# Attention in six groups instead of five, a fourth slot for the sine angles, and new engine orders

## What is computed

```python
y = einsum('bnh,boh->bno', x, weight[subject]) + bias[subject]        # per batch its own weights
q, k, v = heads of y @ Wq.T + bq, y @ Wk.T + bk, y @ Wv.T + bv         # 16 heads of 16
sim = q k^T / sqrt(16) / (|temperature| + 0.1)
scores = sum over 5 frequencies f of alpha[h,f] * sin(2 pi sim / f + phi[h,f])
w = sigmoid(scores); w = w / (sum(w) + 1e-10)
x1 = x + layernorm((w v) @ Wo.T + bo) * gamma + beta
x2 = x1 + relu(x1 @ W1[lang] + b1[lang]) @ W2[lang] + b2[lang]          # adapter per batch
z  = layernorm(x2) * gamma[lang] + beta[lang]
for t in 32 batches:                                                   # recurrence over the batches
    f, i, g = sigmoid(z_t @ wf.T + c @ uf.T + bf), sigmoid(... wi, ui), tanh(... wc, uc)
    c = f * c + i * g
out = x1 + tanh(z @ wo.T + c_final @ uo.T + bo)
```

## Time and profile before

| | |
|---|---|
| Median of 3 runs | 363.52 us (363.08 to 364.91) |
| The profiled execution | 362.38 us, span 360.5 us |
| DVE busy | 302.3 us (84%) |
| PE busy | 296.2 us (82%) |
| ACT busy | 281.9 us (78%) |
| POOL busy | 39.9 us (11%) |
| DMA | 27.55 MB |

### The profile page before, as it was taken

How to read it: one execution, slowest core, us unless ns; L and a number is a source line. 1 busy time by engine, 2 the same in 40 slices (tenths; PEclk the granted TensorE clock), 3 DMA queues, 4 the chain that set the end, 5 groups by cost and what they waited for, 6 DMA issues and landing times.

```text
span 360.5 us, 7287 instructions
## 1 busy us (share of the span) xinstructions
PE 296.2 (82%) x2572; PEld 169.9 (47%) x2572; DVE 302.3 (84%) x661; ACT 281.9 (78%) x407; POOL 39.9 (11%) x49
## 2 busy tenths in 40 slices
PE   5855869577778788798898988998897999998895
PEld 5643348444434455443464545454553434543253
DVE  2379998789988999999799999999999989565344
ACT  1399889599998999999699998999996965322223
POOL 5000930010200001400200011110001301101000
PEclk9999888689989999999899998999999989999999
DMA  6597234553103540034024100220310021000006
GB/s 188 170 276 272 70 91 112 134 154 88 32 18 94 135 141 0 2 96 104 7 73 120 46 4 0 68 64 22 80 38 2 1 86 35 2 0 2 0 12 220
DMA packets 30439, 27.55 MB, mean 76 GB/s; under 512 B 10947, under 2 KB 24387, under 8 KB 30404
## 3 DMA queue, kind: packets, MB, share of 16 engines
q1 hardware_dynamic: 30116, 26.58, 25.4%
q10 hardware_dynamic: 288, 0.53, 0.4%
HBM read 23.16 MB, written 2.10 MB: 70 GB/s over the span
## 4 chain that ended last, share of the span: by engine, by line
DVE 40%; PE 21%; ACT 19%; issue 8%; SPq 7%; POOL 2%; DMA 2%; DVEq 0%; ACTq 0%
DVE sc L1496 12%; ACT ang L1017 6%; DVE ang L1481 5%; PE pg L591 5%; ACT ang L1008 4%; DVE ang L1472 3%; PE pg L584 3%; SPq L295 3%; PE pf L449 2%; PE pr L545 2%; DVE sc L1494 2%; PE pf L507 2%; POOL rs L373 2%; DVE fc L1616 1%; DVE cst L1621 1%
## 5 line engine op out<-in xcount | busy, mean ns | idle before, releaser
L1496 DVE SCALAR_TENSOR_TENSOR sc<-ang,small,sc 128x512 f32<-128x512 f32 (+1 forms) x160 | 98.6, 643 | 1.3
L1017 ACT ACTIVATE ang<-ang,qs 128x2560 f32<-128x2560 int32 x32 | 76.9, 2425 | 1.1 <-DVE ang L1481 0.9
L1008 ACT ACTIVATE ang<-sc,phase 128x512 int32<-128x512 f32 (+1 forms) x126 | 72.5, 641 | 0.0
L584 PE MATMUL pg<-gate_w,zT 128*64 128x384 f32 x256 | 52.5, 519 | 0.9 <-DVE zT L1611 0.9
L591 PE MATMUL pg<-gate_u,cT 128*64 128x384 f32 x256 | 49.6, 510 | 1.8 <-DVE cT L1626 1.8
L1481 DVE TENSOR_SCALAR ang<-ang 128x2560 int32<-128x2560 int32 x32 | 47.7, 1498 | 0.3 <-ACT ang L1008 0.2
L1051 ACT ACTIVATE gat<-pg 128x384 f32<-128x384 f32 x32 | 15.5, 485 | 31.2 <-PE pg L591 31.1
L507 PE MATMUL pf<-qm,kT 64*64 64x128 f32 x512 | 19.9, 298 | 14.0 <-issue 4.5
L1472 DVE TENSOR_SCALAR ang<-sc,phase 128x256 int32<-128x256 f32 (+1 forms) x74 | 28.1, 421 | 1.2 <-ACT sc L999 1.2
L591 PEld LDWEIGHTS pg<-gate_u,cT 128*64 128x64 f32 x256 | 17.5, 142 | 24.3 <-issue 18.4
L584 PEld LDWEIGHTS pg<-gate_w,zT 128*64 128x64 f32 x256 | 16.0, 141 | 20.9 <-issue 17.1
(11 more groups left out here) (125 smaller groups left out, 485.2 us busy)
## 6 DMA issues: line engine op xcount, KB each, us to landing
wc<-in_cond SPq DMA_DIRECT2D x30, 257.0 KB, 3.2
wa<-in_down SPq DMA_DIRECT2D x32, 66.0 KB, 1.9
w<-in_up SPq DMA_DIRECT2D x32, 64.2 KB, 2.2
xt<-in_xt SPq DMA_DIRECT2D x8, 256.0 KB, 3.4
b<-in_up_b SPq DMA_DIRECT2D x32, 64.0 KB, 2.1
out_t<-go SPq DMA_DIRECT2D x8, 256.0 KB, 2.2
xg<-in_x SPq DMA_DIRECT2D x3, 512.0 KB, 4.9
qm<-qT SPq DMA_DIRECT2D x48, 32.0 KB, 2.0
```

Of the source, the lines that this page charges most:

```text
L584: pe.matmul(pg[n % 2][u * L:(u + 1) * L, 0:GCOLS], zT[:, q % 2, kc, t * L:(t + 1) * L], gate_w[:, kc, u, :], start=False, stop=(kc == KC - ...
L1008: op = act.activation(ang[:, n % SLOTS, f, r], unit(n)[:, r], ACT.Identity, scale=TURN / FREQS[f], bias=phase[:, p * NF + f:p * NF + f + 1])
L1017: act.activation(a.bitcast(F32), a, ACT.Sin, scale=2 * PI_LOW / TURN, bias=qs[:, 3:4]).then_inc(sine_ready, 1)
L1496: op = dve.scalar_tensor_tensor(out=unit(n)[:, r], in0=sine, scalar=amp, in1=unit(n)[:, r], op0=ALU.mult, op1=ALU.add)
```

## The change

The third group of 8 batches (20 to 27 of the 32) becomes two groups of 4. SLOTS goes from 3 to 4. ON_ACT falls from 4 to 3 for units 21, 23, 25 and 27. To make room in memory, `rows` loses its fourth plane, `go` keeps only six of eight results and the last two live in `b2` (`kept`). All five lists of calls are new. Of ScalarE's sines and weights, 19 carry True instead of 26.

```diff
-SIZES = (4, 8, 8, 8, 4)
+SIZES = (4, 8, 8, 4, 4, 4)
...
-SLOTS = 3
+SLOTS = 4
...
-ON_ACT = [2, 2, 3, 3, 3, 4, 3, 4, 3, 4, 3, 4, 3, 4, 3, 4, 3, 4, 3, 4, 3, 4, 3, 4, 3, 4, 3, 4, 3, 3, 3, 2]
+ON_ACT = [2, 2, 3, 3, 3, 4, 3, 4, 3, 4, 3, 4, 3, 4, 3, 4, 3, 4, 3, 4, 3, 3, 3, 3, 3, 3, 3, 3, 3, 3, 3, 2]
 ACT_BEFORE = [sum(ON_ACT[:n]) for n in range(B + 1)]
+SPREAD_AT = (0, (GB - SIZES[0]) // PB * PB)
...
-        rows = sb("rows", [P, 4, D])
+        rows = sb("rows", [P, 3, D])
...
-        go = sb("go", [P, 2 * NQ, D])
+        go = sb("go", [P, 2 * (NQ - 2), D])
...
+        def kept(q):
+
+            return go[:, part(q)] if q < NQ - 2 else b2[:, q % 2]
+
...
+            load_rest(1)
+            load_cond(1, 1)
+            load_cond(1, 0)
+            load_x(1)
+            load_cond(1, 2)
             load_cond(1, 3)
-            load_cond(1, 1)
-            load_x(1)
-            load_cond(1, 0)
-            load_cond(1, 2)
             load_rest_consts()
+            spread_q(1, 0)
+            load_cond(2, 1)
             load_x(2)
-            spread_q(1, 0)
             load_rest(0)
             load_cond(2, 0)
             spread_q(1, 1)
             load_cond(2, 2)
-            load_cond(2, 1)
             load_cond(2, 3)
-            load_rest(1)
             load_cond(3, 1)
+            load_rest(2)
             spread_q(2, 0)
             spread_q(2, 1)
-            load_rest(2)
-            load_cond(3, 3)
-            load_cond(3, 2)
+            load_cond(3, 0)
             load_x(3)
-            load_cond(3, 0)
-            load_rest(3)
-            load_cond(4, 1)
+            load_cond(4, 0)
             spread_q(3, 0)
             spread_q(3, 1)
-            load_cond(4, 0)
+            load_rest(3)
             load_rest(4)
             load_x(4)
+            load_cond(4, 1)
+            load_cond(5, 1)
+            spread_q(4, 0)
+            spread_q(4, 1)
+            load_cond(5, 0)
+            load_x(5)
             load_rest(5)
-            spread_q(4, 0)
+            spread_q(5, 0)
             load_rest(6)
-            spread_q(4, 1)
+            spread_q(5, 1)
             load_rest(7)
...
-                                           qm[r * L:(r + 1) * L, b + (c * PB if g == 0 else 0), u, :, :], start=True, stop=True)
+                                           qm[r * L:(r + 1) * L, b + (SPREAD_AT[c] if g == 0 else 0), u, :, :], start=True, stop=True)
...
             output_projection(0, 0)
+            output_projection(0, 1)
             scores(4)
-            output_projection(0, 1)
             scores(5)
+            turn_residual(0)
+            adapter_down(0)
             condition(3, 0)
             condition(3, 1)
-            turn_residual(0)
+            adapter_up(0)
             condition(4, 0)
             condition(4, 1)
-            adapter_down(0)
             turn_tokens(2)
-            adapter_up(0)
...
+            adapter_up(6)
+            turned(7)
+            output_kept(0, 0)
+            output_projection(7, 0)
             turn_normed(6)
-            state_turned(22)
-            turned(7)
-            state_gates(23)
-            output_projection(7, 0)
             output_projection(7, 1)
...
+                if c == 1 and SPREAD_AT[1] == 0:
+                    act.wait_ge(s_done, SIZES[0] // 4)
...
-                act.activation(flat(go[:, part(q)]), src, ACT.Tanh).then_inc(tail_tanh, 1)
+                act.activation(flat(kept(q)), src, ACT.Tanh).then_inc(tail_tanh, 1)
...
             copy_scores(31)
-            gates(17)
             angle(30, 2)
-            residual_turned(5)
             angle(30, 3)
-            turned(6)
-            gates(18)
             angle(30, 4)
             angle(31, 3)
+            angle(31, 4)
+            squares(6)
+            gates(20)
+            sines(30, False)
+            gates(21)
+            sines(31, False)
             weights(28, True)
+            gates(22)
             weights(29, False)
-            angle(31, 4)
-            gates(19)
-            squares(6)
-            sines(30, True)
-            gates(20)
             residual_turned(6)
-            sines(31, False)
-            gates(21)
-            weights(30, True)
-            gates(22)
+            weights(30, False)
             weights(31, False)
+            gates(23)
             keep_output_part(5)
...
             values(1)
             add_sine(4, 0)
             add_sine(4, 1)
             add_sine(4, 2)
             add_sine(4, 3)
-            add_sine(5, 0)
-            add_sine(5, 1)
-            add_sine(4, 4)
-            add_sine(5, 2)
             residual(0)
             residual_added(0)
-            add_sine(5, 3)
-            angle(7, 0)
-            add_sine(5, 4)
+            add_sine(5, 0)
+            add_sine(4, 4)
             base(0)
+            add_sine(5, 1)
+            angle(8, 0)
+            add_sine(5, 2)
             wrap(6)
             shifted(1)
+            hidden(0)
+            angle(8, 1)
...
             add_sine(30, 3)
             add_sine(31, 0)
+            add_sine(30, 4)
+            add_sine(31, 1)
+            cell_step(22)
+            add_sine(31, 2)
+            state_copy(22)
+            add_sine(31, 3)
+            divided(14)
+            add_sine(31, 4)
             base(6)
-            cell_step(21)
-            add_sine(31, 1)
-            state_copy(21)
-            add_sine(31, 2)
-            add_sine(30, 4)
+            hidden(6)
+            divided(15)
             adapted(6)
-            add_sine(31, 3)
             moments(6)
-            add_sine(31, 4)
-            cell_step(22)
+            cell_step(23)
             normalise(6)
-            divided(15)
-            state_copy(22)
             modulated(6)
             shifted_language(6)
-            cell_step(23)
             state_copy(23)
             shifted(7)
             residual(7)
             residual_added(7)
-            base(7)
             cell_step(24)
             state_copy(24)
             hidden(7)
+            base(7)
             cell_step(25)
             state_copy(25)
             adapted(7)
```

More of the change, by code:

```diff
@@ L1265, in _ @@
             angle(22, 3)
-            keep_output_part(1)
-            sines(21, True)
-            turned(3)
             angle(22, 4)
+            angle(23, 2)
+            angle(23, 3)
+            turned(4)
+            residual_turned(3)
+            queries(4, 0)
+            gates(10)
+            sines(22, False)
+            keys(4, 0)
+            weights(20, True)
+            queries(4, 1)
+            keys(4, 1)
+            weights(21, False)
+            angle(23, 4)
+            squares(4)
@@ L1776, in _ @@
+            add_sine(12, 3)
             wrap(13)
-            values(2)
-            add_sine(12, 3)
+            wrap(14)
+            cell_step(3)
+            residual(1)
+            state_copy(3)
+            residual_added(1)
+            add_sine(12, 4)
+            base(1)
             add_sine(13, 0)
-            add_sine(12, 4)
             add_sine(13, 1)
-            angle(14, 0)
-            angle(14, 1)
-            residual(1)
-            residual_added(1)
+            angle(16, 0)
@@ L1829, in _ @@
+            cell_step(4)
+            add_sine(16, 1)
+            state_copy(4)
+            add_sine(16, 2)
+            angle(18, 1)
+            add_sine(16, 3)
+            hidden(2)
+            base(2)
+            divided(6)
             add_sine(16, 4)
-            angle(18, 1)
+            cell_step(5)
+            adapted(2)
+            state_copy(5)
             wrap(17)
-            adapted(2)
-            cell_step(5)
             moments(2)
-            state_copy(5)
+            wrap(18)
@@ L1880, in _ @@
             add_sine(21, 0)
+            shifted(4)
+            state_copy(9)
+            add_sine(21, 1)
+            residual(3)
+            conditioned(4)
+            residual_added(3)
+            angle(23, 0)
+            angle(23, 1)
+            wrap(22)
             add_sine(20, 4)
[L1882 to L1883 removed]
+            add_sine(21, 2)
             cell_step(10)
[L1885 to L1888 removed]
@@ L1889, in _ @@
-            add_sine(21, 4)
-            shifted(4)
-            residual(3)
-            add_sine(22, 0)
-            residual_added(3)
+            hidden(3)
+            base(3)
+            add_sine(21, 3)
+            adapted(3)
+            add_sine(22, 0)
+            moments(3)
+            add_sine(21, 4)
+            add_sine(22, 1)
+            normalise(3)
+            state_copy(10)
+            add_sine(22, 2)
+            wrap(23)
+            modulated(3)
+            residual(4)
@@ L1894, in _ @@
+            shifted_language(3)
+            add_sine(22, 3)
+            add_sine(23, 0)
+            cell_step(11)
+            add_sine(23, 1)
             angle(24, 0)
+            state_copy(11)
             angle(24, 1)
-            add_sine(22, 1)
-            base(3)
-            wrap(23)
-            add_sine(22, 2)
```

(56 more changed lines are left out.)

824 lines of the change are left out of this document (401 added, 423 removed).

## The result

The changed kernel takes 373.71 us (median of 6, 371.86 to 375.96) beside 363.62 us (median of 6) of the kernel before: ratio 1.0286, 95% interval [1.0236, 1.0337], slower by 10.1 us. The forecast was 368.0 with a range of 361.0 to 373.0, so the time lies just above the range and inside what rival C gave (372 at half, 377 at worst). The profiled execution took 375.79 us with a span of 373.9.

A forecast was written before the change was run, and what follows sets the result against it. Both VectorE and ScalarE nearly full up to unit 19, VectorE alone setting the pace from unit 20. +7.6 work - 4.5 idle returned + 1.0 SP queue + 0.4 tail = +4.5 us, median 368.0, range 361.0 to 373.0.

The forecast's parts named there:

- rival C: SP queue becomes the brake: load_x(4) lands 5 us late, load_rest(2) costs 5 more; 377 at worst, 372 at half; chance 0.20.
- the SP queue: load_rest(2) ahead of spread_q(2, 0), load_rest(3) and load_rest(4) ahead of load_x(4): VectorE stall 0 to 10 us, taken as 1.0.
- moves some instructions on and stays: VectorE's 3.5 us stall before 73.24, behind late spread_q(1, 1), was to remain, now before angle(8, 0).
- +7.6 us of VectorE work: VectorE's work before its last attention instruction, add_sine(31, 4): 9.3 from the split, -2.6 moved behind it, +0.9 moved ahead.
- I take 4.5 us back: VectorE idle time returned by fourth slot and new orders: the 2.2 us stall at 177.67 and 2.3 of small waits.
- the second piece: Stretch from 74 to the end of unit 19, where VectorE idled 8.3 us in the kernel before.
- The tail: After add_sine(31, 4): adapted(6) follows it, turn_normed(6) goes between output_projection(7)'s halves; about +0.4 us, bounds 0 and 2.
- load_rest(1) first: At the SP queue's head, delays group 1's weights and x to about 19.1; covered by vz until 28.66, otherwise up to 5 us.
- centre_output_weights later: In the start, centre_output_weights placed after wrap(1): same instructions in another place, counted as nothing.

The follow-up runs named there:

- the split alone: Kernel before, with only the angle and sine steps of units 20 to 27 made two 256-column instructions instead of one of 512, on both engines: 369.51 us, ratio 1.0209.
- the three edits: Changed kernel with load_x(4) and load_cond(4, 1) ahead of load_rest(3) and load_rest(4), load_rest(0) ahead of spread_q(1, 0), centre_output_weights ahead of angle(0, 0): 364.13 us, ratio 1.0054.

## Why the forecast was wrong

**The step that failed** is the SP queue: "bounds for VectorE's stall over both places 0 and 10 us. I take 1.0, near the lower end, because before's later load_rests hid fully behind units of 9 us each". load_x(4) behind two load_rests alone cost 5.2 us (2.4 to 7.9 by the intervals; 5.3 in the traces). The delay was seen and its length was right (22.6 us for the two load_rests, 21.8 in the forecast); what was wrong was the cover. The forecast asked how much slack ScalarE and VectorE have. It should have read TensorE's list, where condition(6, 0) stands ahead of output_projection(3, 1) and state_turned(9), and VectorE's, where state_copy(9) stands ahead of the sums "to go on with". Of the two places the other, load_rest(2), cost next to nothing: between 93 and 200 us no wait of VectorE in the changed kernel is longer than 0.3 us. Moving it behind the spreads cost 11 us.

**The stall that "moves some instructions on and stays"** moved as forecast, to before angle(8, 0), but grew from 3.5 to 5.3 us, since spread_q(1, 1) was issued 8.2 us later than before, not "a little": the forecast counted load_cond(2, 1), but not load_x(2), nor that spread_q(1, 0) could come later. Moving load_rest(0) away was worth 3.0 us here and 3.8 in the kernel before.

**+7.6 us of VectorE work** was nearly right: VectorE's work up to add_sine(31, 4) grew by 6.8. (That the split alone measured 7.6 us is the same figure by chance: its rows gave 6.8.) **"I take 4.5 us back"** was right too, and hidden: without the 5.3 us stall the second piece idles 3.7 us and with the three edits 3.5, where the forecast left 8.3 - 4.5 = 3.8. The causes named bear out: the spread behind load_rest(3) was worth 3.3 us in the kernel before, and seven table loads put back cost 7.6. **The tail**, +0.4, was +0.4, and it is so in seven of the nine profiles of the changed kernel and its variants (55.0 or 55.1 us). **load_rest(1) first** and **centre_output_weights later** were put at nothing but the cover of vz, and moving each back changed nothing; the slot's memory alone changed nothing either.

**The first piece** is 4.1 us longer in the profiled execution, 0.4 of it work and 3.7 idle. values(0) begins 3.4 us later there (30.46 instead of 27.02): 0.8 is a later start and up to 3.0 are matmuls at a lower clock, which this execution happened to have (below). Neither edit of the start moved the median. What the clock does to the medians was not measured apart.

With 5.2 us for the queue instead of 1.0 the sum is 372.2, and with the longer stall about 374, beside the measured 373.7; that it comes so close is partly luck, since the 5.2 is known only to 3 us and the work was 0.8 us less. Rival C had the mechanism and, "372 at half", nearly the time; its chance of 0.20 was too small, because two stalls of this very kind stood in the trace. What stays open is how much of the three-edit kernel's 0.5% is its start: in the profile the start idles 2.2 us more than in the kernel before, and that is within what one start differs from another.

## What to carry to other kernels

When a transfer is moved behind others on a queue, ask first which instruction waits for it, and what stands behind that instruction in the lists of every engine; the slack of the busiest engine is no cover if its own next call waits too. Put long bundles of DMAs where the queue waits for something anyway, and split off the one DMA that is wanted early. In the last attention stage of this kernel, with VectorE 97 to 98% busy, added work was paid nearly in full, and work taken away only turned into waits.

## What was not expected of the hardware

TensorE's granted clock in the first 30 us differs between executions whose TensorE work up to there is the same. values(0, .), 32 matmuls, takes 1.97 us in some and 3.3 to 3.7 in others. The kernel before and the changed one, timelines of TensorE:

```profile
18.61 1.10 PE L427 MATMUL pf<-yT,wq 128*128 128x256 f32 x4 [1.30 <-ACT sc L999]
...
24.61 1.97 PE L483 MATMUL pf<-wv,yT 128*64 128x128 f32 x32 [1.65 <-ACT sc L999]
```

```profile
19.38 1.81 PE L435 MATMUL pf<-yT,wq 128*128 128x256 f32 x4 [1.30 <-ACT sc L1014]
20.98 1.91 PE L435 MATMUL pf<-yT,wk 128*128 128x256 f32 x4
...
27.02 3.33 PE L491 MATMUL pf<-wv,yT 128*64 128x128 f32 x32 [1.47 <-ACT sc L1014]
```

Over values(0, .) the mean granted clock is 1.00 in the first (24.61 to 26.58) and 0.57 in the second (27.02 to 30.35). The lower of the two levels, 1.2 GHz instead of 2.4, lies over different stretches of the start: over the second projections and values in the changed kernel, and in one more, over values alone in nine others (of both orders), over the projections alone in one, and over neither in five. In the two above TensorE had waited the same 1.3 us before the projections, so these rows do not show what made it fall. VectorE's values(0) comes at 27.0 to 30.6 accordingly, 27.0 to 29.0 with the old order of calls and 27.1 to 30.6 with the new one. So 2 us of one profiled start are chance with either order, and up to 3 us where both stretches are slow. A first stretch should not be read from one execution.
